# Borders between the stages of a six-layer transformer block: attention and feed-forward passes take turns

## The reference

```python
x = x + tanh(g_ffn[0]) * L0_ffn(layernorm(x), ...)

def L0_ffn(x, ...):
    for i in range(DEPTH):                       # 6 layers
        x = attn_layer(shift_tokens(x), Wqkv[i], q_scale[i], k_scale[i], Wo[i]) + x
        x = ffn_layer(shift_tokens(x), ln_g[i], ln_b[i], W1[i], b1[i], W2[i], b2[i]) + x
    return x
# attn_layer: q, k, v of 16 heads of 64; q and k normalised, rotary tables; attention in a
#   window of 32 with its predecessor; softmax; product with Wo
# ffn_layer: layer norm, W1 to 2 x 341, a * gelu(gate), W2
# shift_tokens: the second half of the features comes from the token before
```

## Time and profile before

| | us |
|---|---|
| median of 3 runs | 4849.04 (4835.33 to 4851.96) |
| the profiled execution | 4846.29 |
| its span, first to last instruction | 4844.4 |
| attention, full passes | 14.395 each |
| layer to layer (first Y addition of layers 0 to 5) | 571.6, 573.3, 572.5, 569.5, 571.8 |
| mean granted clock of PE | 0.946 |

### The profile page before, as it was taken

One profiled execution on the slowest core, in us unless ns is written; L12 is line 12 of the kernel. 1 busy time (PEld: TensorE's weight loads), 2 busy tenths in 40 slices (PEclk: granted clock), 3 DMA queues, 4 the chain that ended last, 5 costly groups with the idle time before them and its releaser, 6 DMA issues.

```text
span 4844.4 us, 147943 instructions
## 1 busy us (share of the span) xinstructions
PE 4316.4 (89%) x51751; PEld 2925.7 (60%) x51751; DVE 3484.6 (72%) x7330; ACT 2577.7 (53%) x5842; POOL 2801.1 (58%) x3445
## 2 busy tenths in 40 slices
PE   4999978999899988999889998899889998688799
PEld 3777764555655566555655556555565556466565
DVE  3666657887588866888678885888768886666566
ACT  2555545666366654666456664666546665355322
POOL 1333337887288854888458882788638885255300
PEclk9999999999899999999999998999999999787589
DMA  2000000000100000000100001000010000100000
GB/s 78 7 6 6 6 21 10 4 5 5 41 5 5 4 26 20 5 5 6 31 13 5 4 6 40 5 4 5 7 40 4 5 4 12 32 12 12 3 7 11
DMA packets 160436, 64.06 MB, mean 13 GB/s; under 512 B 121364, under 2 KB 155936, under 8 KB 159520
## 3 DMA queue, kind: packets, MB, share of 16 engines
q1 hardware_dynamic: 160288, 62.05, 4.9%
HBM read 26.54 MB, written 2.10 MB: 6 GB/s over the span
## 4 chain that ended last, share of the span: by engine, by line
POOL 45%; PE 28%; issue 22%; DVE 2%; POOLq 1%; SPq 1%; ACT 1%; DVEq 0%; DMA 0%; ACTq 0%
POOL big L503 9%; POOL qn L503 9%; POOL e L498 8%; POOL big L492 7%; POOL qn L492 6%; PE pj L1460 3%; PE pj L1303 3%; PE pp L1261 2%; PE sc L1472 2%; PE po L1276 1%; PE turn L1460 1%; PE sc L1619 1%; PE pj L1295 1%; PE pj L1344 1%; PE po L1282 1%
## 5 line engine op out<-in xcount | busy, mean ns | idle before, releaser
L1361 PE MATMUL pj<-wqkv,xcT 128*128 128x512 f32 x1536 | 841.0, 631 | 17.4 <-DVE big L939 9.5
L503 POOL TENSOR_TENSOR big<-big 128x512 f32<-128x512 f32 x384 | 485.0, 1272 | 306.2 <-DVE big L939 306.2
L503 POOL TENSOR_TENSOR qn<-qn,big 128x512 f32<-128x512 f32 x384 | 486.3, 1277 | 207.2 <-DVE big L939 207.2
L643 ACT ACTIVATE big<-pj 128x512 f32<-128x512 f32 x768 | 459.4, 598 | 269.7 <-PE pj L1361 216.0
L939 DVE TENSOR_TENSOR big<-pj,ropes 128x512 f32<-128x512 f32 x768 | 522.2, 680 | 0.0
L944 DVE TENSOR_REDUCE ss<-big 128x8 f32<-128x512 f32 x768 | 503.9, 677 | 0.0
L1449 PEld LDWEIGHTS pp<-wo,oT 128*128 128x128 f32 x3072 | 367.1, 196 | 154.6 <-issue 146.0
L498 POOL TENSOR_TENSOR e<-e,rc 128x512 f32<-128x512 f32 x384 | 399.8, 1042 | 58.2 <-DVE rc L974 58.2
L1449 PE MATMUL pp<-wo,oT 128*128 128x128 f32 x3072 | 404.2, 286 | 7.0 <-ACT oT L666 7.0
L492 POOL TENSOR_TENSOR qn<-qn,ny 128x512 f32<-128x512 f32 x384 | 392.1, 1042 | 14.8 <-POOL ny L524 13.4
L938 DVE TENSOR_TENSOR qn<-pj,ropec 128x512 f32<-128x512 f32 x384 | 262.5, 684 | 191.2 <-ACT big L643 153.6
(11 more groups left out here) (297 smaller groups left out, 9480.9 us busy)
## 6 DMA issues: line engine op xcount, KB each, us to landing
wqkv<-in_L_ffn_Wqkv SPq DMA_DIRECT2D x6, 1536.0 KB, 6.3
xsd<-Y SPq DMA_DIRECT2D x192, 32.0 KB
xsd<-Y SPq DMA_DIRECT2D x384, 15.8 KB
xsf<-Y SPq DMA_DIRECT2D x96, 64.0 KB
xsf<-Y SPq DMA_DIRECT2D x192, 31.5 KB
xsx<-Y SPq DMA_DIRECT2D x64, 64.0 KB, 1.8
xsx<-CT SPq DMA_DIRECT2D x64, 64.0 KB, 1.9
wo<-in_L_ffn_Wo SPq DMA_DIRECT2D x6, 512.0 KB, 7.4
```

Of the source, the lines that this page charges most:

```text
L503: nc.gpsimd.tensor_tensor(U[a.par][i], U[a.par][i], t2b[i % 2], ALU.add).then_inc(sem("d_add"), 1)
L643: nc.scalar.activation(sqb[i % 2], pj[i % 2][:, :], ACT.Square).then_inc(sem("d_sq"), 1)
L1361: mm(pj[i % 2][:, :], xcT[:, a.par, :], wqkv[:, i * 512:i * 512 + 512], start=True, stop=True).then_inc(sem("d_ch"), 1)
```

## The change

`stream` is no longer used for the two pipelines. `layers` writes one order of passes that PE, DVE, ACT and POOL all follow. With d for this layer's attention passes, f for feed-forward passes and d' for the next layer's attention passes, a layer is now:

d3 to d30 (a loop of two), d31, d32, **f0, d33, f1, f2, f3, d34**, f4 to f15 (a loop of two), f16, **d'0, f17, d'1, f18, d'2**.

The loop over layers runs five times, and the last layer follows it, written out. `gate` holds the waits that each engine needs ahead of certain passes, and the rotary tables of DVE and the table load of ACT. To let both kinds of passes be under way at once, some buffers change: the third hidden product goes to `sc[:, 512:1024]` instead of `pt_`, the W2 products to `sc[:, 0:512]` and `po[0]` instead of the two halves of `sc`, the transposition of feed-forward to `pt_` instead of `pp`, gelu's output to `qn` instead of `e`. SP loads rounds 0 to 3, not 0 and 1, ahead of the next layer's attention weights; the rest of its order stays. The instructions themselves, their number and shapes are the same.

```diff
-        f_hid = [pj[0], pj[1], pt_]
+        f_hid = [pj[0], pj[1], sc[:, 512:1024]]
+        f_out = [sc[:, 0:512], po[0]]
...
+        def passes(n, body, base, hbase, ks, stages=4):
+
+            for k in ks:
+                body(*(Tile(base + (k - s), k - s, (k - s) % 2, hbase + (k - s) // 2) if 0 <= k - s < n else None for s in range(stages)))
...
+            def layer(l, more):
+                k = full_passes(eng, NT, d_body, l * NT, l * (NT // 2), 3)
+                d_pass(l, *range(k, NT + 1))
+                f_pass(l, 0)
+                d_pass(l, NT + 1)
+                gate("f1", l)
+                f_pass(l, 1)
+                gate("f2", l)
+                f_pass(l, 2, 3)
+                d_pass(l, NT + 2)
+                gate("f4", l)
+                k = full_passes(eng, NF, f_body, l * NF, l * (NF // 2), 4)
+                f_pass(l, *range(k, NF + 1))
+                if more:
+                    gate("d0", l)
+                    d_pass(l + 1, 0)
+                f_pass(l, NF + 1)
+                if more:
+                    gate("d1", l)
+                    d_pass(l + 1, 1)
+                f_pass(l, NF + 2)
+                if more:
+                    gate("d2", l)
+                    d_pass(l + 1, 2)
+
+            gate("first", 0)
+            d_pass(0, 0, 1, 2)
+            with eng.Fori(0, DEPTH - 1) as l:
+                layer(l, True)
+            layer(DEPTH - 1, False)
...
                 ffn_weights(l)
                 both_slots(2, NT, attention_tile, l * NT)
-                for r in range(2):
-                    ffn_round(l * NF + r, r, r)
+                for r in range(4):
+                    ffn_round(l * NF + r, r, r % 2)
                 if l + 1 < DEPTH:
                     attention_weights(l + 1)
-                both_slots(2, NF, ffn_round, l * NF)
+                both_slots(4, NF, ffn_round, l * NF)
...
-            with pool.Fori(0, DEPTH) as l:
-                stream(pool, NT, d_body, l * NT, l * (NT // 2), 4)
-                stream(pool, NF, f_body, l * NF, l * (NF // 2), 4)
+            layers(pool, d_body, f_body, lambda name, l: None)
...
+                if name == "first":
+                    pe.wait_ge(sem("att_loaded"), ATT_LOADS)
+                    pe.wait_ge(sem("y_ready"), NT)
+                elif name == "f1":
+                    past(pe, "d_tc", l * (4 * NT) + 4 * NT)
+                elif name == "f2":
+                    pe.wait_ge(sem("ffn_loaded"), l * FFN_LOADS + FFN_LOADS)
+                    past(pe, "d_vc", l * (2 * NT) + 2 * NT)
+                elif name == "f4":
+                    past(pe, "d_oc", l * (2 * NT) + 2 * NT)
+                    past_waits(pe, "went_on")
+                elif name == "d0":
+                    past(pe, "f_xT", l * NF + NF)
+                elif name == "d1":
+                    pe.wait_ge(sem("att_loaded"), l * ATT_LOADS + 2 * ATT_LOADS)
+                    past(pe, "f_hT", l * (3 * NF) + 3 * NF)
+                elif name == "d2":
+                    pe.wait_ge(sem("y_ready"), l * NT + 2 * NT)
```

More of the change, by code:

```diff
@@ L301, in stream, with full_passes, layers, d_pass @@
                 body(*(tile(k - s) if k - s < n else None for s in range(stages)))
+        def passes(n, body, base, hbase, ks, stages=4):
+            for k in ks:
+                body(*(Tile(base + (k - s), k - s, (k - s) % 2, hbase + (k - s) // 2) if 0 <= k - s < n else None for s in range(stages)))
+        def full_passes(eng, n, body, base, hbase, first, stages=4):
+            turns = (n - first) // 2
+            with eng.Fori(0, turns) as i:
+                for k in range(first, first + 2):
+                    body(*(Tile(i * 2 + base + (k - s), i * 2 + (k - s), (k - s) % 2, i + hbase + (k - s) // 2) for s in range(stages)))
+            return first + 2 * turns
+        def layers(eng, d_body, f_body, gate):
+            def d_pass(l, *ks):
+                passes(NT, d_body, l * NT, l * (NT // 2), ks)
+            def f_pass(l, *ks):
+                passes(NF, f_body, l * NF, l * (NF // 2), ks)
+            def layer(l, more):
[27 more added lines that the diff above has]
+            layer(DEPTH - 1, False)
         def head_start(eng, *names):
@@ L713, in gelu @@
                         past(act, "f_hT", c.g * 3 + (j - 2))
-                        nc.scalar.activation(e[0:n, j, 0:256], f_hid[j][0:n, 0:256], ACT.Gelu, bias=fb1[0:n, 1, j:j + 1]).then_inc(sem("f_gl"), 1)
+                        nc.scalar.activation(qn[0:n, j, 0:256], f_hid[j][0:n, 0:256], ACT.Gelu, bias=fb1[0:n, 1, j:j + 1]).then_inc(sem("f_gl"), 1)
                 gelu(0)
@@ L1029, in f_body @@
                     ds = bass.ds(d.t * FT, FT)
-                    nc.vector.tensor_tensor(Y[:, ds, :], sc[:, d.par * 512:d.par * 512 + 2 * D].rearrange("p (a d) -> p a d", a=2), Y[:, ds, :], ALU.add).then_inc(sem("y_ready"), FT)
+                    nc.vector.tensor_tensor(Y[:, ds, :], f_out[d.par][:, 0:2 * D].rearrange("p (a d) -> p a d", a=2), Y[:, ds, :], ALU.add).then_inc(sem("y_ready"), FT)
                 if a:
@@ L1035, in f_body, with rope_tables @@
                 gated(2)
-            with dve.Fori(0, DEPTH) as l:
+            def rope_tables(l):
                 dve.wait_ge(sem("att_loaded"), l * ATT_LOADS + ATT_LOADS)
@@ L1047, in _, with gate @@
                 dve.wait_ge(sem("tables"), l + 1)
-                stream(dve, NT, d_body, l * NT, l * (NT // 2), 4)
-                dve.wait_ge(sem("ffn_loaded"), l * FFN_LOADS + FFN_LOADS)
-                stream(dve, NF, f_body, l * NF, l * (NF // 2), 4)
+            def gate(name, l):
+                if name == "first":
+                    rope_tables(0)
+                elif name == "f2":
+                    dve.wait_ge(sem("ffn_loaded"), l * FFN_LOADS + FFN_LOADS)
+                elif name == "d0":
+                    rope_tables(l + 1)
+            layers(dve, d_body, f_body, gate)
             dve.wait_ge(sem("y_ready"), NT * (DEPTH + 1))
@@ L1458, in hidden @@
                         past(pe, "f_hT", c.g * 3 + (j - 2))
+                        if j == 2 and isinstance(c.t, int) and c.t == 0:
+                            past(pe, "d_sub", c.g * (2 * NT // NF) + 2 * NT)
                         for k in (1, 0):
@@ L1471, in f_body @@
                             k = n + (j == 2)
-                            last = mm(sc[:, s0 + i * D:s0 + i * D + D], hT[0:k, d.par, j, i * P:i * P + P], fw2[0:k, j, :], start=(j == 0), stop=(j == 2))
+                            last = mm(f_out[d.par][:, i * D:i * D + D], hT[0:k, d.par, j, i * P:i * P + P], fw2[0:k, j, :], start=(j == 0), stop=(j == 2))
                     last.then_inc(sem("f_y"), 1)
@@ L1477, in f_body, with gate @@
                     for i in range(FT):
-                        last = nc.tensor.transpose(pp[:, i * P:i * P + P], fxn[:, i * P:i * P + P], ident)
+                        last = nc.tensor.transpose(pt_[:, i * P:i * P + P], fxn[:, i * P:i * P + P], ident)
                     last.then_inc(sem("f_xnT"), 1)
                 hidden(2)
[L1482 to L1491, removed]
+            def gate(name, l):
+                if name == "first":
+                    pe.wait_ge(sem("att_loaded"), ATT_LOADS)
+                    pe.wait_ge(sem("y_ready"), NT)
+                elif name == "f1":
+                    past(pe, "d_tc", l * (4 * NT) + 4 * NT)
+                elif name == "f2":
+                    pe.wait_ge(sem("ffn_loaded"), l * FFN_LOADS + FFN_LOADS)
[3 more added lines that the diff above has]
+                    past_waits(pe, "went_on")
+                elif name == "d0":
+                    past(pe, "f_xT", l * NF + NF)
+                elif name == "d1":
+                    pe.wait_ge(sem("att_loaded"), l * ATT_LOADS + 2 * ATT_LOADS)
+                    past(pe, "f_hT", l * (3 * NF) + 3 * NF)
+                elif name == "d2":
+                    pe.wait_ge(sem("y_ready"), l * NT + 2 * NT)
+            layers(pe, d_body, f_body, gate)
             def l_body(a, b, c, d, e_):
```

22 lines of the change are left out of this document (10 added, 12 removed).

## The result

The changed kernel takes 4872.97 us (median of 5 runs, 4869.09 to 4876.62), the kernel before, timed beside it, 4849.04: ratio 1.0055, 95% interval 1.0038 to 1.0072. It is slower by 24 us, as forecast in direction and inside the range, but only a little over half of the 41 us between the forecast of 4890 and that median.

What follows compares the result with a forecast made beforehand. PE, busy 89% of the span, was taken to bound the kernel, with slack only at the two layer borders. Terms 40.3 + 1.3 + 2 = 43.6 us on 4846.3 gave about 4890 us, range 4855 to 4925.

Steps and rivals of the forecast that it cites:

- Step 1: First border, f0 ahead of d33: POOL's addition and power wait for DVE's statistics, so d33 starts 4.1 us later.
- Step 3: First border, f1 to f3 ahead of d34: POOL's last softmax products stand behind three powers, a 12.79 us chain.
- Step 4: First border, d34 itself: 11.68 us before, 1.4 us taken off for a higher PE clock, output products still low.
- Step 5: First border, load for f4: waits behind d34 and four weight loads, 8.7 us, making f4's statistics 8.1 us later.
- Step 6: After f4's wait: PE being ahead against a slow clock start, taken as 0, bounds -1.8 and +1.8 us.
- the first border: From tile 29's Y addition to round 4's statistics: 8.1 us later in each of five layers, 40.3 us.
- The last layer: Its first border, without weight loads: +1.3 us, 1 us of it for hidden products that come behind d34 on PE.
- The second border: Feed-forward end to next layer's attention: 5.6 us gain lost waiting for tile 2's load; +2 us over five borders.
- DVE's branch: Second border, now between d'2 and d'3: fetching its target idles DVE; d'3 starts 0.4 to 0.6 us later, four layers.
- The passes really overlap: Rival, first border: POOL takes the last tile's products before the powers of f1 to f3; 4802 us, chance 0.09.
- The clock stays high: Rival, both borders: PE idles less at a stretch, so half-rate parts run at full rate; 4853 us, chance 0.07.
- Only the second border pays: Rival: tile 2's load is not late, so 5.6 us each stay at the second border; 4862 us, chance 0.07.

Runs made afterwards that it cites:

- a_pool: Changed kernel with POOL's order alone edited: f0's addition and power come behind d33's norms and products; ratio 1.0007 to the kernel before.
- a_split: Changed kernel with d34 cut into four pieces that alternate with f1, f2 and f3, loads unchanged; ratio 0.9975 to the kernel before.
- a_rounds6: Changed kernel with SP issuing rounds 0 to 5, not 0 to 3, ahead of the next layer's attention weights; ratio 0.9986 to the kernel before.
- only_first: Changed kernel with f17 and f18 put back ahead of d'0, so only the first border is interleaved; ratio 1.0046 to the kernel before.
- old_loads: Kernel before, with SP issuing rounds 0 to 3 ahead of attention weights and tiles 0 to 3 ahead of feed-forward weights; ratio 1.0005 to the kernel before.
- a_r6t4: Changed kernel with SP issuing six rounds ahead of the attention weights and four tiles ahead of the feed-forward weights; ratio 0.9935 to the kernel before.

## Why the prediction was right, and where its sizes were off

**Step 1** held: POOL begins d33 at +2.2 us relative to tile 29's Y addition instead of -1.9, the 4.1 us of the forecast. Of these 3.3 us reach the Y addition of tile 30. `a_pool` takes it away and wins 3.7 us at the border in the mean: a wait of one small instruction at the head of a queue.

**Step 3** held: the chain from there to POOL's last power takes 12.0 us in the mean of five layers, where 12.8 were taken from the last layer's rows. `a_split` shows that the two chains could have run side by side and do not in this order.

**Step 4**: 10.4 us in the mean, 10.3 forecast, and that is partly luck. The guess on the clock, high at first and low for the output products, fits four layers (10.6 to 11.4 us). In layer 3 and in the last it was high throughout, and d34 took 8.4 us. The reason given, that the gaps between the groups stay, does not decide it: the gaps were the same in all six, 1.16 us ahead of the output products.

**Step 5** is the main point and held: 9.2 us from the end of the output products to f4's statistics, 8.7 forecast, 8.23 of them idle on DVE. `a_rounds6` removes the wait by moving the load; a shorter one of 2.1 to 3.1 us appears in f6, and 31 us are gained all the same.

**Step 6** was about right at 0: f4's statistics came 6.9 us late in the mean, round 8's addition 7.2. Together the first border was forecast at 8.1 and measured 7.2: 5 us too many over five layers. Steps 1 and 3 were each 0.8 us too long, step 5 was 0.5 too short.

**The last layer** was wrong in sign: +1.3 forecast, -2.4 measured. The largest term is step 4's, 10.3 us there against 8.4. The 1 us for f4's products behind d34 cost nothing that shows: DVE took up the statistics 0.9 us after the output products. The rest, under 1 us, lies ahead of d34.

**The second border** was the larger error: +0.4 forecast, -2.3 measured, 14 us over five layers. The mechanism is the one forecast, PE waits for tile 2 behind f18 and the weights; the term that was mis-sized is the load. I added 9.0 us of issuing and 1.9 of landing; in all five layers the transposition starts 9.1 us after the last W2 product. SP's issues show where, first the old kernel, then the changed one:

```profile
2448.78 3.57 SPq L361 DMA_DIRECT2D fb<-in_L_ffn_b  x6
```

```profile
2485.32 2.49 SPq L417 DMA_DIRECT2D fb<-in_L_ffn_b  x6
...
2489.09 1.68 SPq L434 DMA_DIRECT2D xsd<-Y  x2
```

The six small bias loads took 1.1 us less to issue, and the load landed 1.2 us after its last issue (2490.77 to 2491.94) instead of 1.9, which I had taken from the load of a round, twice as large. This is 1.8 of the 2.7 us. The quicker issue is not the interleaving's doing: `only_first`, with the second border in the old order, has 2.50 us as well.

```profile
2467.01 2.50 SPq L416 DMA_DIRECT2D fb<-in_L_ffn_b  x6
```

For the rest the forecast had the starting point right (d'1's first rotary product, the end of f18) but took no account of a border that is 1 to 2 us shorter even in the old order, as `only_first` shows.

DVE's branch behaves as forecast: idle 3.38 us with no semaphore to explain it (3.4 to 3.5 in four layers), 0.85 us of it beyond what ACT's square would have asked for; at the fifth border, without the branch, it was 1.90. The Trainium skill ("Runtime: NRT & Kernel Launch", Instruction fetch mechanics) puts such idleness down to fetching the branch's target; the trace agrees that it stands behind the branch to the layer loop and not behind the branches of the short loops, where DVE has no idleness without a semaphore above 0.15 us.

**The rivals.** "The passes really overlap" did not happen; POOL's order decided it, as said. "The clock stays high" had a part: the granted clock rose from 0.946 to 0.953 on the whole, and from 0.72 to 0.81 at the first border, but the output products still ran at the lower level in four of six layers. "Only the second border pays" was right in that it is shorter, wrong in that the interleaving did it.

## What to carry to other kernels

Before two pipelines are interleaved pass by pass, write down for each queue, the DMA-issuing one too, which instruction stands ahead of each moved one and what that one waits for: here a two-element power, three small powers and a weight load cost more than the overlap gave. Move the loads along with the passes; two more rounds and two more tiles ahead of the weights gave nothing in the old order and 59 us in the new one. The two chains bound by latency at the first border overlapped only when they alternated step by step (`a_split`), not pass by pass.

## What the runs showed of the hardware that was not expected

The issue time of identical small DMAs varied: the six bias loads took 3.6 to 4.2 us in the kernel before and 2.5 in all the others, `old_loads` among them, which has the old order of passes but issues them 10 us later. In the kernel before they fall together with DVE's idleness behind the branch to the next layer (it lasts until 2450.91, the issues from 2448.78 to 2452.35). That the one causes the other is not shown.

Right after dense feed-forward products PE's clock stayed high for the transpositions and most of the products with v (0.66, 0.63, 1.75 us against 0.90, 1.09, 2.12), and was at the lower level for the output products 1.2 us later (3.78 us at a granted clock of 0.50). In `a_split`, where no gap preceded them, they took 1.95 us in all six layers. But behind the same gap of 1.16 us they also took 2.05 us at 1.00, in two of the six layers of the change and in all six of `a_r6t4`. What settles the level behind such a gap these rows don't tell; it moves d34 by 2 to 3 us, as much as some of the terms of the forecast.
